# One or two identity products in place of three at each of 24 fixed turns of TensorE

## The reference

```python
h = tok_ref(x, ...)                       # 3 gathered rows of 75, gate softmax, sum of 3 products
h = h + attn0(_layernorm(h), ...)         # qkv, tanh/sin/cos features, kv state, layernorm, out
h = h + ffn0(_layernorm(h), ...)          # weights W1 + sum_e g_e tv_W1[e], relu, layernorm
h = h + attn1(_layernorm(h), ...)         # q, k scaled by cumulative gates, causal, no softmax
h = h + ffn1(_layernorm(h), ...)          # top 2 of 8 experts, gelu
```

## Time and profile before

| | |
|---|---|
| time, median of 3 launches | 376.22 us (373.08 to 377.03) |
| the profiled launch, its own time | 375.65 us |
| its span, first to last instruction | 373.6 us |
| mean granted clock of TensorE | 0.99 |
| busy: TensorE matmul, VectorE, ScalarE, GpSimd | 92%, 74%, 57%, 31% |
| matmul records of the N turns | 144 (72 products) |

### The profile page before, as it was taken

The page is one execution under the profiler, slowest core; times in us unless marked ns, Lnnn a source line. Parts: engine busy times, 40 slices in busy tenths (PEclk is TensorE's granted clock), DMA queues, the critical chain, the costliest instruction groups (busy, mean ns, idle before and its releaser), DMA issues.

```text
span 373.6 us, 9934 instructions
## 1 busy us (share of the span) xinstructions
PE 342.3 (92%) x3309; PEld 268.9 (72%) x3309; DVE 277.4 (74%) x901; ACT 213.9 (57%) x496; POOL 117.1 (31%) x127
## 2 busy tenths in 40 slices
PE   2898877899999999999999999997797999999995
PEld 1666867458543998348975569754696999999994
DVE  1768787898999894598898998799864674344366
ACT  1248585495567945454375255572348758578661
POOL 6861020140200500200030133527621177477600
PEclk9999996999999999999999999999999999999999
DMA  5699999300000000000000049101112113341172
GB/s 132 168 415 370 310 288 288 87 0 1 2 0 3 1 4 4 0 0 3 4 0 2 3 135 344 34 0 45 53 45 61 46 52 94 85 134 57 33 255 84
DMA packets 25032, 33.98 MB, mean 91 GB/s; under 512 B 4674, under 2 KB 19786, under 8 KB 24600
## 3 DMA queue, kind: packets, MB, share of 16 engines
q1 hardware_dynamic: 22200, 27.52, 24.0%
q0 software_dynamic: 2784, 5.84, 4.9%
HBM read 19.14 MB, written 14.40 MB: 90 GB/s over the span
## 4 chain that ended last, share of the span: by engine, by line
PE 66%; DVE 17%; issue 6%; ACT 4%; DMA 3%; POOL 3%; POOLq 0%; DVEq 0%; ACTq 0%; SPq 0%
PE bank L958 6%; PE bank L1102 6%; PE bank L1091 6%; PE bank L899 4%; PE bank L919 4%; PE bank L940 4%; PE bank L912 4%; PE bank L952 4%; PE bank L1049 3%; PE bank L1042 3%; PE bank L992 2%; PE bank L1004 2%; PE bank L973 2%; PE bank L840 2%; POOL experts_out L762 2%
## 5 line engine op out<-in xcount | busy, mean ns | idle before, releaser
L1354 ACT ACTIVATE ht<-bank,arena 128x128 f32<-128x128 f32 x156 | 43.9, 371 | 13.2 <-PE bank L1091 11.9
L1102 PE MATMUL bank<-big,ht 128*128 x312 | 40.7, 277 | 1.1 <-ACT ht L1354 0.9
L754 POOL DMA_INDIRECT dealt<-xy,arena x32 | 32.3, 1008 | 25.9 <-DVE arena L1727 15.7
L1102 PEld LDWEIGHTS bank<-big,ht 128*128 128x128 f32 x312 | 37.5, 192 | 1.9 <-issue 1.9
L762 POOL DMA_INDIRECT experts_out<-arena x27 | 27.6, 1023 | 12.5 <-issue 7.0
L958 PE MATMUL bank<-xT_f,wq 128*128 128x512 f32 x64 | 29.7, 596 | 0.0
L744 POOL TENSOR_TENSOR arena<-arena 128x8 f32<-128x8 f32 x4 | 6.7, 1671 | 52.8 <-DVE arena L1650 40.4
L1613 DVE TENSOR_TENSOR_SCAN lb<-la 128x512 f32<-128x512 f32 x16 | 19.5, 1216 | 3.8 <-ACT la L1287 2.0
L958 PEld LDWEIGHTS bank<-xT_f,wq 128*128 128x128 f32 x64 | 11.6, 190 | 12.0 <-issue 11.2
L1122 PEld LDWEIGHTS bank<-ident 128*128 128x128 f32 x144 | 18.5, 204 | 1.2 <-issue 1.0
L727 POOL TENSOR_TENSOR xn_d<-xn_d,wide 128x512 f32<-128x512 f32 x4 | 5.1, 1275 | 45.5 <-DVE wide L1557 45.5
(11 more groups left out here) (314 smaller groups left out, 906.0 us busy)
## 6 DMA issues: line engine op xcount, KB each, us to landing
dealt<-w1s SPq DMA_DIRECT2D x3, 1768.5 KB, 16.7
big<-in_tv SPq DMA_DIRECT2D x2, 2048.0 KB
big<-in_ew SPq DMA_DIRECT2D x16, 256.0 KB, 6.1
dealt<-w1s SPq DMA_DIRECT2D x2, 1572.0 KB, 22.8
arena<-dealt SPq DMA_DIRECT2D x27, 65.5 KB, 1.8
wq<-in_wq SPq DMA_DIRECT2D x1, 1024.0 KB, 16.8
vv<-experts_out SPq DMA_DIRECT2D x2, 512.0 KB, 5.0
out<-h SPq DMA_DIRECT2D x3, 256.0 KB, 2.8
```

The source lines that it names most:

```text
L754: pool.indirect_dma_start(xs, bass.IndirectOffsetOnAxis(ap=goal[b][:, k, t:t + 1], axis=0), xy[b % 2][:, k, t, :], None).then_inc(s_deal[b ...
L1102: last = pe.matmul(p[:, 0:D], hid[n % DEEP][:, c * P:(c + 1) * P], big[:, bass.ds(e * FF + (E * FF + c * D), D)], start=(c == 0), stop=(c ...
L1354: last = act.activation(hid[n % DEEP][:, c * P:(c + 1) * P], of("K.up", n)[:, c * P:(c + 1) * P], ACT.Gelu, bias=eb1[:].rearrange("p e c - ...
```

## The change

Turn n holds 1 + n % 2 products, so even turns hold one and odd turns two. The 24 turns hold 36 products instead of 72. Nothing else changes: the turns, their places, their wait and the bank stay.

```diff
             def section_N(n, ph):
                 pe.wait_ge(s_gatev, 1)
-                for i in range(3):
+                for i in range(1 + n % 2):
                     pe.matmul(bank[7][:, 0:P], ident[:], ident[:], start=True, stop=True)
```

## The result

| | before | after |
|---|---|---|
| median of all launches | 376.62 us (373.08 to 377.88, 4) | 382.18 us (380.71 to 382.92, 4) |
| profiled launch, own time and span | 375.65, 373.6 us | 380.71, 378.7 us |
| mean granted clock of TensorE, profiled | 0.990 | 0.968 |

The changed kernel is slower: its ratio to the kernel before is 1.016, with a 95% interval of 1.010 to 1.022. The median of 382.18 us lies just above a forecast range that ended at 382.0; the profiled launch, 380.71 us, was the fastest of the four. The ratios in this text leave out the launches that are more than 1.5% above the fastest of their kernel, and in the kernel before those are the ones with the longest stretches at the low clock, so the median of all launches stands beside each ratio.

What follows compares the result with a forecast made beforehand. The prediction took VectorE and ScalarE to bound the chain up to 66 us, identity products being off it. 375.65 + 0 + 2.0 + 1.3 + 0 = 378.95 us, plus 0.57 for the median: 379.5 us, slower by 0.9%, range 375.2 to 382.

Steps and rivals of the forecast that it cites:

- What bounds the kernel: Up to 66 us the chain runs over VectorE and ScalarE between TensorE's real work; removing 8.5 us of products gains 0.
- The one turn at 127 us: Behind 120 us only six records of identity products, of which two go; no gain was counted for them.
- Rests: TensorE's idle times ahead of L795, L811 of batch 1, L831 and L869 grow to 2.9, 2.4, 3.8 and 3.0 us.
- Term 1: First T chain, 16.46 to 21.25 us: L795, L804, L806, L811 run at the low clock; +2.0 us, bounds 0 and 2.6.
- Term 2: Stage C of batch 0 (L831 to L840), 39.92 to 42.78 us, partly at the low clock: +1.3 us, bounds 0 and +2.5.
- Term 3: Stage C of batch 1, from 60.01 us, already low and staying so: 0, bounds -2.5 and +0.5 us.
- rival C: Low stretch at 54 to 65 us moves off stage C of batch 1: -2.5 us, 373.5 us; chance 0.07.
- the later work: From 120 us on, dense and at clock 1.00 throughout, hardly touched by the change; early delays pass on without slack.
- rival D: More stages hit: both early terms at their upper ends, 5.1 us, plus a tail at batch 1; 381.3 to 383 us; chance 0.10.
- The base line: Profiled launch of 375.65 us; the low stretch at 58.6 us, worth 2.5 to 3 us, about matches the launches' 4 us range.
- The rule cited: The chip judges the clock free of the kernel's start, so slow products vary by launch; the changed kernel would scatter more.

Runs made afterwards that it cites:

- e3: The kernel before with no products in any of the 24 turns, their wait kept: 381.0 us, against 376.73 us for before beside it.
- e2: The changed kernel with three products again in the eight turns on both sides of L822 of batch 1: 377.81 us, before beside it 376.73 us.
- e6: The kernel before with five more turns of three products in three late rests of TensorE: 374.26 us, before beside it 374.98 us.
- e5: The changed kernel with five more turns of three products in three late rests of TensorE: 378.81 us, kernel before beside it 374.98 us.
- e7: The kernel before with five late and eight early turns of three products added in idle time: 373.57 us, before beside it 374.98 us.
- e12: The kernel before with fifteen more products behind the turn at 127.5 us, a shift of 3.5 us: 378.37 us, before beside it 375.28 us.
- e9: The kernel before with nine more products behind the turn at 127.5 us, shifting later work 2.1 us: 380.62 us, before beside it 377.1 us.
- e13: The changed kernel with six more products behind the turn at 127.5 us: 378.43 us, kernel before beside it 375.28 us.
- e11: The kernel before with five late and eight early turns added and the turn at 127.66 us taken out: 373.29 us, before beside it 377.1 us.
- e8: The kernel before with all 72 products kept, each streaming 2 columns instead of 128: 382.31 us, before beside it 374.98 us.

## Why the prediction missed

**What bounds the kernel: right in direction.** No identity product of the first 66 us was in the chain, and taking all of them out (e3) gave nothing back. That TensorE idles after nearly every run of them is not so: in the timeline before, up to 57 us, it did after four of ten runs (1.32, 1.23, 0.63 and 2.33 us). The one turn at 127 us is in it. The prediction put it at nothing; it was worth 0.3 us in the changed kernel for one product of three.

**Rests: right.** 2.9, 2.4, 3.8 and 3.0 us were forecast, 3.72, 2.47, 3.90 and 3.00 came. The first was longer because the run began and ended earlier than reckoned (11.38 to 13.29 us) and L795 was let go 0.55 us later.

**Term 1, +2.0 us: +1.2.** L795 and L804 ran low as forecast, L806 and L811 didn't. The trace's record of the clock begins with a rise at 13.6 us, so it had risen after all; it fell at the end of the rest and was back at 20.4 us, earlier than the 21.2 us taken from the rows.

**Term 2, +1.3 us: +2.5.** The bound was right, the choice within it wrong. The delay of 1.35 us between the end of a rest and the fall, seen once, was carried over to a rest that is 1.6 us longer. The clock fell during the rest, ahead of L831, and not after it. e2 shows that this term hangs on the eight turns around L822.

**Term 3, 0: -2.0.** The low stretch moved from stage C of batch 1 to L869 and L811 ahead of it, of which only a part is in the chain. That is rival C's mechanism at less than its full price. The three early terms sum to 1.7 us and, with the later start, to 2.3; the forecast had 3.3. This is against a launch of before that had an early low stretch itself; against one without, as e6 and e5 show, the early part costs 4.6 us.

**The step that failed** is the sentence on the later work, "dense and at 1.00 throughout, and the change hardly touches it". The one row that it rested on showed a mean clock of 1.00 over 254 us of one launch, and the rests of 1.73, 0.96 and 1.79 us near 250 to 265 us were not looked at. The prediction put the later work at 0. Low stretches there cost 3.5 us in the profiled launch (2.9 and 0.6), and with the rests filled (e5) they are gone. No term or rival reached beyond 120 us, and the sum came out 2.7 us too low; rival D got near the time for another reason. That the stretches come from the rests is shown. Why the changed kernel has them every time and the kernel before in about half of its launches is not.

**The base line** was a launch in the middle of a mixture. The prediction read the spread of before as one low stretch at 58.6 us. The 72 launches show more: those at 372.9 us have the clock at 0.999 or 1.000, and those at 377 to 380 us have it down longer, as the launches with late stretches do. With the late rests filled (e6) the slowest of ten launches took 375.2 us, where before reached 380.4. The early stretches and some spread at a clock of 1.0 (e7, up to 374.1 us) make up the rest.

**The rule cited** from the Trainium skill, TensorE: Matmul & The Clock Gate, Part 1, What's actually happening, that the chip's judging runs free of the kernel's start, fits the scatter of before, the first rises at 11.9 to 15.0 us, and the equal rests at 255.1 us with and without a fall (changed kernel and e12). The result drawn from it, that the changed kernel would scatter more, was wrong: its four launches lie within 2.2 us, those of before within 4.8. Whether e9, e12 and e13 show a dependence on where the late rests lie in time, which the rule alone wouldn't give, is open.

## What to carry to other kernels

Work that exists to keep TensorE's clock up has to be judged rest by rest, over the whole span and not only where it stands: list every idle time of TensorE, ask what stands behind it in the chain, and price that stage at both levels of the clock. Look at the mean clock of many launches before trusting one profile; if it differs from launch to launch, the gain is in filling the rests that remain, as e11 did, and a change that only shifts later work can win or lose some microseconds with no cause in the work that it touches. Fill a rest only up to its own length: six products a turn cost more than none.

## What the runs showed of the hardware

- With 2 columns instead of 128 in every identity product, TensorE was busy for 3.83 us ahead of the first T chain and the clock was still low at 16.1 us; the median was 382.3 us, like that of the changed kernel (e8).
- Rests of 1.73 and 1.79 us were followed by a fall in some launches and not in others. After the same rest of 1.73 us, ended at the same 255.1 us, the clock fell in the profiled launch of the changed kernel and not in that of e12.
- The first rise of the clock in the profiled launches came at 12 to 15 us or, in e3, e5, e8 and e13, only at 20 to 22 us. The latter four have four full products, none, or narrow ones in the first run; with four it also came at 13.6 us (changed kernel) and 11.9 us (e2).
